# Attention: both halves of a head group's probability-value product on TensorE at every fourth step

## What is computed

```
qkv = x @ qkv_w.T + qkv_b                      # 16 heads of 8 features
attn = softmax(einsum('bhqd,bhkd->bhqk', q, k) * SCALE)
out  = einsum('bhqk,bhkd->bhqd', attn, v)      # the product of probabilities and values
out  = out.reshape(b, n, dim) @ out_w.T + out_b
```

```
x = x + attn_a(layernorm(x))
x = x + ffn(layernorm(x))       # shared expert + top 2 of 8 routed experts
x = x + attn_b(layernorm(x))    # the attention above
x = x + ffn(layernorm(x))
```

## Time and profile before

| what | value |
|---|---|
| time, median of 3 runs | 867.91 us (865.51 to 868.33) |
| time of the profiled execution | 864.54 us |
| span in its trace, first to last instruction | 862.7 us |
| mean granted TensorE clock | 0.910 |
| PE busy over the span | 685.2 us (79%) |
| DVE busy | 646.9 us (75%) |
| ACT busy | 526.3 us (61%) |
| POOL busy | 478.7 us (55%) |

### The profile page before, as it was taken

One profiled execution on the slowest core, in us unless ns is written; L12 is line 12 of the kernel. 1 busy time (PEld: TensorE's weight loads), 2 busy tenths in 40 slices (PEclk: granted clock), 3 DMA queues, 4 the chain that ended last, 5 costly groups with the idle time before them and its releaser, 6 DMA issues.

```text
span 862.7 us, 22793 instructions
## 1 busy us (share of the span) xinstructions
PE 685.2 (79%) x7807; PEld 488.3 (57%) x7808; DVE 646.9 (75%) x1433; ACT 526.3 (61%) x1236; POOL 478.7 (55%) x496
## 2 busy tenths in 40 slices
PE   1265289699999906889989989997989949999980
PEld 1233289588898903334434444443438939888980
DVE  7979969477777443889989888987766228888748
ACT  3366364276676504588889788877775526666640
POOL 3987315677876277848227206003577737777740
PEclk9999569899999955699989998998899969999995
DMA  7222110033335111101000000000011322333236
GB/s 193 73 74 31 46 54 2 25 78 88 91 85 79 47 49 46 32 8 35 17 2 2 2 1 2 2 2 2 21 53 57 108 58 74 86 82 90 74 106 198
DMA packets 62745, 46.88 MB, mean 54 GB/s; under 512 B 8771, under 2 KB 57067, under 8 KB 62680
## 3 DMA queue, kind: packets, MB, share of 16 engines
q1 hardware_dynamic: 53592, 28.02, 12.1%
q0 software_dynamic: 9088, 17.98, 8.2%
HBM read 26.76 MB, written 20.13 MB: 54 GB/s over the span
## 4 chain that ended last, share of the span: by engine, by line
PE 57%; DVE 25%; ACT 6%; issue 5%; POOL 5%; DMA 2%; SPq 0%; DVEq 0%; ACTq 0%; POOLq 0%
PE ps L877 30%; PE ps L1021 12%; DVE mx L2226 6%; PE ps L1255 5%; DVE xn L1720 4%; PE ps L1036 3%; POOL rows L827 3%; DVE xres L2123 2%; PE ps L1113 2%; POOL gy L756 2%; PE ps L1268 1%; ACT scratch L1590 1%; DVE rnorm L1748 1%; DVE hlo L2219 1%; DVE hl L1727 1%
## 5 line engine op out<-in xcount | busy, mean ns | idle before, releaser
L1466 ACT ACTIVATE h<-ps,b1T 128x256 f32<-128x256 f32 x440 | 171.9, 479 | 56.8 <-PE ps L877 56.8
L2226 DVE TENSOR_REDUCE mx<-ps 128x2 f32<-128x512 f32 x256 | 171.9, 687 | 30.6 <-PE ps L877 29.1
L1590 ACT ACTIVATE scratch<-ps 128x512 f32<-128x512 f32 x256 | 149.4, 603 | 37.7 <-PE ps L877 36.3
L877 PE MATMUL ps<-xg,w1s 128*128 128x256 f16 x936 | 117.9, 277 | 11.4 <-issue 9.5
L1021 PE MATMUL ps<-w2s,hhi 128*128 x1248 | 117.3, 219 | 0.0
L838 POOL DMA_INDIRECT ytok<-yst,didx x78 | 89.5, 1148 | 42.9 <-DVE yst L2057 22.2
L877 PE MATMUL ps<-kst,qst 32*128 32x256 f16 x512 | 97.5, 290 | 10.6 <-DVE mx L2226 10.3
L742 POOL DMA_INDIRECT scratch<-rows,tok_i x78 | 89.9, 1153 | 26.8 <-issue 23.2
L1492 ACT ACTIVATE xg<-ps 128x512 f16<-128x512 f16 x78 | 46.5, 597 | 95.1 <-PE ps L1113 95.1
L877 PEld LDWEIGHTS ps<-xg,w1s 128*128 x936 | 88.5, 99 | 25.7 <-issue 15.5
L1999 DVE SCALAR_TENSOR_TENSOR hlo<-h,hhi 128x1024 f16<-128x1024 f32 x78 | 95.6, 1225 | 2.7
(11 more groups left out here) (310 smaller groups left out, 1345.7 us busy)
## 6 DMA issues: line engine op xcount, KB each, us to landing
gy<-rows SPq DMA_DIRECT2D x39, 136.0 KB, 2.2
ysorted<-yst SPq DMA_DIRECT2D x39, 128.0 KB, 1.9
h<-in_L_ffn_ew SPq DMA_DIRECT2D x16, 256.0 KB, 3.1
scratch<-ytok SPq DMA_DIRECT2D x16, 256.0 KB, 3.4
xres<-in_L_attn_a_x SPq DMA_DIRECT2D x4, 512.0 KB, 6.1
rows<-hl SPq DMA_DIRECT2D x4, 512.0 KB, 3.3
out_x<-xres SPq DMA_DIRECT2D x4, 512.0 KB, 4.3
scratch<-rows,tok_i POOLq DMA_INDIRECT x78, 2.8
```

Of the source, the lines that this page charges most:

```text
L877: return pe.matmul(o, a, b, start=start, stop=stop)
L1466: last = act.activation(h32[:, u % 2, f], HB[u % 2][:, f], ACT.Gelu_apprx_tanh, bias=b1T[:, ds(e * CH + c, 1)], scale=1.0 / PS)
L1590: act.activation(prb[:, (s // 4 * 4 + (s + 2) % 4) % 8, :], ps[:, s % 2, :], ACT.Exp, scale=HD ** -0.5 / (PS * PS))\
L2226: dve.tensor_reduce(mx[:, c, j:j + 5:4], ps[:, 2 + s % 2, :].rearrange("p (n k) -> p n k", n=2), AX_X, ALU.max).then_inc(Att.mx, 1)
```

## The change

Both halves of a group stand together: groups 0, 1 and 2 behind scores 6, 10 and 14, and group 3 behind scores 1 of the next batch. Within a step they still come first, ahead of what else stands there. No instruction is added or taken away, and no wait is new in the text of the other engines.

```
-                    if output and s in (1, 2):
-                        weigh(b - 1, 1 - u, 3, s - 1)
+                    if s == 1 and output:
+                        weigh(b - 1, 1 - u, 3, 0)
+                        weigh(b - 1, 1 - u, 3, 1)
                     if s == 1 and output:
                         turn_back(body, b - 1, 0)
...
-                    if s >= 5 and s % 2 == 1:
-                        weigh(b, u, (s - 5) // 4, (s - 5) // 2 % 2)
+                    if s in (6, 10, 14):
+                        weigh(b, u, (s - 6) // 4, 0)
+                        weigh(b, u, (s - 6) // 4, 1)
                     if s == 5 and ahead:
                         values(body, b + 1)
```

## The result

The changed kernel takes 884.73 us (883.07 to 886.12, 4 runs) against 868.12 us (865.51 to 868.59, 4 runs) of the kernel before on the same chip: a ratio of 1.0192, 95% interval 1.0147 to 1.0237. The forecast was 876, with a range of 867.5 to 883.0: the sign is right, the loss is twice as large, and the median lies 1.7 us above the range. The profiled execution took 883.07 us with a span of 881.3 us; that is +18.5 us and +18.6 us on the profiled execution before.

The account below looks back on a forecast made before the run. PE was taken to lead by 8%, with DVE's row maxima holding part of the chain. Terms of 5.5, 1.6, 1.6 and 0 gave +8.7, taken as +8 on the median 867.91: 876 us, range 867.5 to 883.

Parts of the forecast that it names:

- the plain batch: Batches 2, 3, 4, 6 and 10: each longer by 1.1 us on 15.9, 5.5 us together.
- the wait ahead of `maxima` of step 3: Steps 1 to 3 of a plain batch: with half 2 gone, PE idles about 0.6 us for `normalise`.
- steps 7 to 9: Plain batch, up to `maxima` of step 9: +0.03 us, with PE idle 0.6 us where half 9 stood.
- wait for maximum 11: Plain batch, ahead of scores 13: PE is ready before DVE's maximum 11 is over, +0.18 us.
- scores 15 to scores 1: End of a plain batch: scores 1 of the next batch wait for maximum 15, 1.17 us later, about +0.30.
- steps 9 to the next `turn_back`: Last part of a plain batch: 0.10 us of PE work, 0.52 of new waits, 0.43 from group 3's pair.
- the way to the end: Delays of batches 0 to 13 reach the end one to one; those of batches 14 and 15 fall into 11.72 us idle.
- batches 7, 8, 11, 12: PE already waits for DVE behind step 6, so the pair fills this wait: about +0.4 us each, 1.6 together.
- a pair behind scores 6 is hidden in that: Batches 1, 5, 9, 13: PE's 0.83 us wait behind a table load hides the pair; +0.4 us each, 1.6 together.
- batch 0 at nothing: Batch 0 has no link to a batch before, so it was taken to lose 0 us.
- fourth rival: New idle stretches lower the clock in two or three more places, each losing up to 3.5 us: 883 us; chance 0.08.
- second and third rivals: Second: PE alone decides, 8 us saved, 860 us, chance 0.12. Third: no change, 865.3 to 870.5 us, chance 0.20.

Follow-up runs that it names:

- e1: Kernel before with only group 3's halves paired, in step 1, groups 0 to 2 as before; ratio 0.9895 to the kernel before.
- e2: Kernel before with only groups 0 to 2 paired, behind scores 6, 10 and 14, group 3 as before; ratio 1.0153 to the kernel before.
- e7: Changed kernel with group 1 alone put back to single halves, behind scores 9 and 11; ratio 1.0243 to the kernel before.
- e8: Changed kernel with group 2 alone put back to single halves, behind scores 13 and 15; ratio 1.0141 to the kernel before.
- e13: Kernel before with small matmuls added inside TensorE's waits of step 3 in batches 1, 5, 9 and 13; 868.33 us against 869.32.
- e14: Changed kernel with small matmuls added inside TensorE's waits of step 3 in batches 1, 5, 9 and 13; 873.95 us, ratio 1.0063 to the kernel before.
- e12: The changed kernel measured again, unaltered, on another chip; ratio 1.0208 to the kernel before.
- e15: Changed kernel with groups 0 to 2 of batch 0 placed as in the kernel before; 884.4 us, one execution.
- e6: Kernel before with the changed order only in batches 1, 5, 9 and 13; ratio 1.0132 to the kernel before.
- e5: Changed kernel with batches 1, 5, 9 and 13 in the order of before; ratio 1.0163 to the kernel before.

## Why the prediction was wrong

**Right: the plain batch.** Forecast +1.1 us, measured +1.19 in batches 3 and 4 (sum of the five: 4.8 for 5.5). Its terms, forecast and measured: the pair 1.00 and 1.00 to 1.01; the wait ahead of `maxima` of step 3 0.6 and 0.62, nothing lost between `turn_back` and there; steps 4 to 7 +0.05 and +0.05; steps 7 to 9 +0.03 and +0.04; wait for maximum 11 0.18 and 0.23; scores 15 to scores 1 1.17 and 1.17; steps 9 to the next `turn_back` +1.05 (0.10, the waits' 0.52, the pair's 0.43) and +1.09. e1, e2, e7 and e8 give the shares by group.

**Right: the way to the end.** What batches 0 to 13 lose arrives one to one behind POOL's sends, and batch 15's 4.9 us are hidden.

**Too small: batches 7, 8, 11, 12.** Forecast 1.6, measured 2.8. The lateness of steps 1 to 3 is won back by step 7 as forecast (-0.46 us in batch 8), but the last segment then grows by 1.09 us as in a plain batch: 0.68 in sum, where the forecast's own terms give 0.62 and it took 0.4. In batches 11 and 12 the last segment grows by 1.3; batch 12 also has 3.3 us at 1.2 GHz after and none before. I did not separate the two.

**The step that failed: "a pair behind scores 6 is hidden in that, so I take +0.4 each, 1.6, between 0 and 1.1".** Batches 1, 5, 9 and 13 grew by 8.25 us. I had read the one wait of the earlier trace rows, in batch 13, and carried it to all four. What the runs show in its place:

- Batches 5 and 9, 1.94 and 1.95 us: in the kernel before the wait does not exist there, because PE works at the 0.50 of the earlier trace rows and everything else is ahead of it. What I took as a resource that hides the pair was an engine at half speed that hides nothing. At half clock a pair takes 1.87 us where the two halves took 1.02 + 0.65, and scores 6 and 7 stand apart. At full clock the batches grow by 0.37 us each (e13, e14), which is near my 0.4 partly by luck: e13's last segment is 0.77 us longer than batch 1's, with the wait on POOL in it, which the forecast did not know. That is also why the lower clock costs the kernel before so little: its last segment is 7.79 us, and 8.56 at full clock; after, it is 9.24 and 9.23. In numbers, 1.94 = 0.37 + (2.82 - 1.25).
- Batch 1, 1.23 us: here the wait exists (0.81 us, at full clock), and the pair does hide in a part of it. But what follows is not hidden: the last segment grows by 1.44 us. At full clock the batch grows by 0.9 us (e12; e13 and e14), so the term was too small there without any change of clock; the other 0.3 us goes with 3.3 us at 1.2 GHz.
- Batch 13, 3.13 us: below.

**Also off: batch 0 at nothing.** It runs at 1.2 GHz for its first 11 us in the kernel before. The first pair of the changed one falls into that (at 360.75, it lasts 1.94 us where one at full clock lasts 1.07), and the time at 1.2 GHz grows to 14.4 us; it is +1.69 us, with group 3's pair of step 1. e15 speaks for 1.0 of it as the price of its own pairs.

**Batch 13 and the fourth rival.** Batch 13 is +3.13 us, with 20.5 us at 1.2 GHz for 10.0. The changed code at full clock takes 20.53 us there (e14), so the clock costs it 6.5 us. Whether the pairs brought that on is not shown: with pairs the batch ran at full clock in e2, e6, e7, e8 and e15, and without them (e5) it had 20 us at 1.2 GHz. The order of before was not seen at full clock in this batch; the nearest is e1, 19.91 us with 3.4 us at 1.2 GHz, so, as an estimate, at least some 0.6 us of the 3.13 would be there at full clock too. As an estimate from these rows, the change costs 17.5 - 8.25 + 0.9 + 2 x 0.37 = 10.9 us up to batch 14, and what batch 13 costs, where these four batches stay at full clock; the forecast's 8.7 was low for that as well.

The fourth rival, to which I gave 0.08, said: the lower clock in two or three more places of about 7 us, 883 us. The extra 20 us at 1.2 GHz are just that amount, and 883.07 us is what the profiled execution took. That is luck, for its reason was wrong. The idle stretches of 0.6 us in plain batches brought no lower clock anywhere: batches 2, 3, 4, 6, 7, 8, 10 and 11 are at 1.00 in the trace after. It is lower in batches 0, 5, 9 and 13, where it was lower before, for longer or at a higher price, and for 3.3 us each in batches 1 and 12. What sets how long it stays down is open; e5, e6 and e15 show that it is not the code of the batch itself.

**The second and third rivals** asked that the halves lost as cover cost less than the 0.56 us saved in a batch, or that slack take up the waits. Neither is seen: a plain batch loses 1.19 us net. The saving itself is there. The Trainium skill (TensorEngine Tiling (Array Packing), Key Properties) says that a change of tiling mode drains TensorE. The trace fits it, with 1.00 us for a pair and 1.14 for two halves apart; no run here tells a drain from another cost of the change.

## What to carry to other kernels

An instruction that stands in an engine's wait is free only there; merging two such pieces to save a switch moves one out of its cover, and here a plain batch saved some 4 x 0.14 us and was still 1.19 us longer. That a wait hides the step itself is not enough: follow the lateness to the batch's end (batch 1 hid it and still grew by 0.9 us). Before you say that a wait will hide a step, look at the granted clock of that very stretch: at half clock the engine that you take to be waiting may be the late one, and a wait seen in one batch must not be carried to others. Where the clock is unsteady, sum the batches at full clock apart from those at half, and give the latter a range of their own.

## What the runs showed of the hardware

- In batches 5 and 9 the granted clock fell to 0.50 within 0.2 us of PE's wait of 2.14 us or inside it, and stayed there for 7 us (before, after and e12), or for 14 and 20 us (e15). After, e12 and e15 have the same instructions in the same order there. With this wait unfilled the clock fell in 25 of 26 cases over all runs.
- In batch 13 the changed kernel waits 1.34 us, and the clock fell 1.7 us behind that wait for 20 us; in e15, with the same wait, it stayed at 1.00:

```profile
607.81 0.40 PE L877 MATMUL ps<-ident,hlo 128*128 128x128 f16 x4 [1.34 <-DVE h L2246]
```

- With PE's waits of 0.55 and 0.62 us the clock stayed at 1.00 in all five plain batches of the changed kernel.
- With 29 small matmuls in and ahead of the wait of 2.14 us, which left 0.69 us of it idle, the clock stayed at 1.00 in batches 5 and 9 of both kernels. The changed kernel with them takes 873.95 us, for 884.73 and 884.4 without; the kernel before takes 868.33 for 869.32, nothing that can be told, since its clock fell in batches 12 and 13 instead.
- A pair of 16 matmuls takes 1.00 us at 2.4 GHz and 1.87 us at 1.2 GHz.
